# Four attention layers on one core: when pieces of x and the second layer's weights are loaded

## What is computed

```python
x = _L0_xattn_ref(x, ctx, mask, ...)   # q k v projections, softmax(q k^T / 4) v, @ Wo.T, + x, layernorm
x = _L1_xattn_ref(x, ctx, ctx, ...)    # the same with other weights
x = _L2_xattn_ref(ctx, x, ...)         # layernorm + causal self-attention, layernorm + cross-attention,
                                       # layernorm + relu feed-forward 256 -> 1024 -> 256
x = _L3_xattn_ref(x, ctx, ...)         # layernorm, ternary weights (bit_quant), cross-attention, + x
```

## Time and profile before

| | us |
|---|---|
| median of 3 runs | 1397.14 (1395.04 to 1398.23) |
| the profiled execution | 1397.33 |
| its span in the trace | 1395.6 |
| PE busy | 1329.5 (95%) |
| DVE, ACT, POOL busy | 994.2, 898.1, 603.0 |

### The profile page before, as it was taken

One profiled execution on the slowest core, in us unless ns is written; L12 is line 12 of the kernel. 1 busy time (PEld: TensorE's weight loads), 2 busy tenths in 40 slices (PEclk: granted clock), 3 DMA queues, 4 the chain that ended last, 5 costly groups with the idle time before them and its releaser, 6 DMA issues.

```text
span 1395.6 us, 46148 instructions
## 1 busy us (share of the span) xinstructions
PE 1329.5 (95%) x20076; PEld 1138.8 (82%) x20076; DVE 994.2 (71%) x1842; ACT 898.1 (64%) x1519; POOL 603.0 (43%) x767
## 2 busy tenths in 40 slices
PE   5999999999999999999999999999999999899997
PEld 4777888777887878888788878888999999778885
DVE  4778777888788777767776788886664446767774
ACT  4777777777777756666566776776434435667764
POOL 4944544576644643443334342222686665111100
PEclk9999999999999999999999999999999999999999
DMA  7211100010100000000000110000000000001000
GB/s 283 76 31 35 31 13 10 24 31 25 38 9 9 10 25 3 3 2 2 3 2 25 33 31 16 9 9 24 9 9 1 2 1 15 10 32 39 17 25 32
DMA packets 16609, 35.11 MB, mean 25 GB/s; under 512 B 2071, under 2 KB 7447, under 8 KB 15895
## 3 DMA queue, kind: packets, MB, share of 16 engines
q1 hardware_dynamic: 16407, 32.16, 7.1%
HBM read 27.96 MB, written 4.19 MB: 23 GB/s over the span
## 4 chain that ended last, share of the span: by engine, by line
PE 67%; DVE 14%; ACT 8%; POOL 5%; issue 3%; DMA 2%; SPq 0%; DVEq 0%; POOLq 0%; ACTq 0%
DVE s_nm L1101 9%; PE ps L717 8%; PE ps L782 8%; PE ps L744 6%; PE ps L796 6%; PE ps L810 6%; PE ps L606 5%; PE ps L659 5%; PE ps L761 5%; PE ps L631 4%; ACT s_PU L952 4%; PE ps L618 4%; PE ps L595 2%; PE ps L722 2%; DVE s_KH L1058 2%
## 5 line engine op out<-in xcount | busy, mean ns | idle before, releaser
L1101 DVE TENSOR_REDUCE s_nm<-ps 128x8 fp32r<-128x960 f32 (+1 forms) x352 | 395.8, 1168 | 88.4 <-PE ps L659 51.0
L952 ACT ACTIVATE s_PU<-ps 120x1024 f32<-120x1024 f32 (+1 forms) x288 | 280.6, 1024 | 105.5 <-PE ps L722 105.3
L717 PE MATMUL ps<-s_Qs,s_KH 32*120 32x256 f32 (+2 forms) x4608 | 184.8, 288 | 6.4 <-ACT s_PU L952 2.6
L1225 POOL TENSOR_TENSOR s_xs<-s_xs,s_rowv 128x512 f32<-128x512 f32 x96 | 123.9, 1291 | 151.8 <-ACT s_nt L857 133.6
L717 PEld LDWEIGHTS ps<-s_Qs,s_KH 32*120 32x120 f32 (+1 forms) x4608 | 151.5, 181 | 28.4 <-issue 5.1
L1254 POOL TENSOR_SCALAR s_rs<-s_mv 128x2 f32<-128x2 f32 x96 | 23.2, 242 | 325.4 <-DVE s_mv L1138 319.8
L961 ACT ACTIVATE s_Os<-ps 128x512 f32<-128x512 f32 x160 | 95.0, 598 | 102.8 <-PE ps L744 64.2
L782 PE MATMUL ps<-s_W,s_oT 128*128 128x256 f32 x960 | 135.3, 291 | 5.2 <-DVE s_oT L1030 3.5
L606 PE MATMUL ps<-s_xT,s_W 128*128 128x256 f32 x960 | 135.9, 292 | 3.1 <-POOL s_xT L1231 2.8
L744 PE MATMUL ps<-s_PU,s_Vp 120*32 120x256 f32 x2048 | 129.5, 384 | 9.2 <-ACT s_PU L952 7.2
L782 PEld LDWEIGHTS ps<-s_W,s_oT 128*128 128x128 f32 x960 | 120.0, 190 | 16.8 <-DVE s_oT L1030 7.0
(11 more groups left out here) (96 smaller groups left out, 2554.4 us busy)
## 6 DMA issues: line engine op xcount, KB each, us to landing
s_cf<-ctx_t SPq DMA_DIRECT2D x32, 240.0 KB, 2.6
s_ws<-weights SPq DMA_DIRECT2D x28, 256.0 KB, 2.7
s_nt<-x_t SPq DMA_DIRECT2D x16, 256.0 KB, 2.6
s_xs<-x_nat SPq DMA_DIRECT2D x4, 1024.0 KB, 11.3
out<-s_xs SPq DMA_DIRECT2D x16, 256.0 KB, 2.0
s_rowv<-rows SPq DMA_DIRECT2D x6, 512.0 KB, 3.9
s_mi<-mask SPq DMA_DIRECT2D x8, 120.0 KB, 3.4
s_who<-who SPq DMA_DIRECT2D x1, 128.0 KB, 3.2
```

Of the source, the lines that this page charges most:

```text
L717: e.matmul(banks[j][0:n, wide * x:wide * x + wide], kz[row[j], lk, g, c, k0:k0 + n], q[row[j], lq, g, qs_], start=(x == 0 and y_ == 0), st ...
L952: t = e.activation(P_of(i, k)[0:n, :, :], pair("B", i, k)[0:n, :, :], ACT.Exp, scale=0.25)
L1101: e.tensor_reduce(o, v, AX.X, ALU.max, negate=True).then_inc(sem["max"])
L1225: e.tensor_tensor(xs[:, b, :, :], xs[:, b, :, :], row2(layer, 0), ALU.add).then_inc(sem["pool"])
```

## The change

Two lists of predecessors are added in the planner and two settings are replaced.

- Piece 0 of x is put behind stage K.0, and piece k behind stage A of item 4k - 4 (A.0, A.4, A.8).
- Quarter m of L1's weights is put behind A of item 4 + m.
- All of `WANT` (the due-time offsets of every stage in every layer) is replaced, and `STAY` goes from 0.236 to 0.224.

No stage, no instruction of a stage and no semaphore wait is written anew.

```diff
-WANT = dict(Xl=-8.6, xT=-3, cT=-4, mi=-4, bo=(-0.05, 0.32, 4.13, 3.45, 8.95, -1.6), N=(0, 0, 6.16, 6.96, 8.36, 7.97),
...
+WANT = dict(Xl=-16.43, xT=-3, cT=-4, mi=-4, bo=(0.97, -1.34, -3.22, 0.61, 12.29, -3.48), N=(0, 0, 10.64, 12.42, 13.44, 15.82),
...
-STAY = 0.236
+STAY = 0.224
...
     for k in range(4):
-        p.add("SP", "x", k, want=-1 + 1.2 * k)
+        p.add("SP", "x", k, want=-1 + 1.2 * k, after=[("A", 4 * k - 4, 0)] if k else [("K", 0, 0)])
...
         for m in (1, 0, 2, 3) if n == 0 else range(4):
             at = start + .5 * m if n else {1: -9, 0: -3.9, 2: -2.7, 3: -.5}[m]
-            p.add("SP", "ws", layer, m, want=at, rings=[("ws", (layer, m), [(rest_of(layer), layer, m)])])
+            p.add("SP", "ws", layer, m, want=at, after=[("A", 4 + m, 0)] if layer == "L1" else [], rings=[("ws", (layer, m), [(rest_of(layer), layer, m)])])
```

More of the change, by code:

```diff
@@ new lines @@
+WANT = dict(Xl=-16.43, xT=-3, cT=-4, mi=-4, bo=(0.97, -1.34, -3.22, 0.61, 12.29, -3.48), N=(0, 0, 10.64, 12.42, 13.44, 15.82),
+            T=(0, 0.13, 0.21, -0.79, -0.22, 0.31), Q=(1.81, 1.08, 0.96, 0.51, 0, 1.71), Qh=(-0.74, 0.6, -6.57, -3.9, 0, 0.97),
+            Ql=(-0.59, 3.99, 10.39, 2.06, 0, 1.73), K=(2.63, 1.19, -2.71, -0.39, 0, 0.98), Kh=(0.11, -16.63, 4.49, 3.4, 0, 0.76),
+            Kl=(5.54, 8.06, 1.45, 6.65, 0, 7.2), K0=(-13.91, 8.99, 3.75, -3.34, 0, -10.45), V=(3.07, 1.25, 1.38, 0.83, 0, 1.91),
+            Ve=(1.65, -1.23, 1.72, -2.43, 0, -2.35), mf=13, A=(0.29, -1.85, -1.85, -0.06, 0, -3.8),
+            max=(9.11, -12.31, -2.63, -4.61, 0, -2.63), M=(-16.49, -3.61, -3.9, -2.29, 0, -18.15),
+            mTe=(11.14, 12.03, -0.16, 11.27, 0, 8.12), B=(-7.63, -1.62, -2.03, 0.48, 0, -9.14),
+            exp=(-3.12, 14.76, -1.95, 3.12, 0, 13.36), cap=-12.12, PV=(2.26, -0.16, -0.07, 1.54, 0, 1.6),
+            PVe=(-3.45, 1.58, -1.77, 10.39, 0, -0.05), ON=(4.19, 1.38, 3.31, 2.6, 0, -2.95),
+            ONe=(-1.24, -7.63, -1.04, -2.21, 0, -8.35), OT=(3.58, -9.96, 2.54, 2.48, 0, 5.52), O=(-7.31, -5.09, 0.12, 1.33, 0, 1.98),
+            y=(3.96, -9.58, -3.69, 15.16, 2.84, 1.03), st=(5.2, 11.02, 19.36, 14.14, 14.68, 0),
+            rs=(9.18, -8.49, -2.17, -8.62, -2.02, 0), ln=(8.94, -0.06, 0, 0, 0, 0), lng=(-25.75, -16.59, 0, 0, 0, 0), F1=-0.24,
+            Fa=-8.05, Fv=21.82, Hl=-3.15, F2=2.37, out=2.2, Th=(-4.04, -13.24, -7.11, -0.2, -8.86, -15.35),
+            Tl=(0, -2.6, 4.26, -6.59, -10.81, -3.43), OTh=(-15.58, -4.22, -23.32, 2.17, 0, -4.46),
+            OTl=(-2.73, 3.61, 0.93, -0.17, 0, -5.85), Ch=(11.16, 3.48, 0, 4.99, 0, -6.26), Cl=(-7.06, 0.87, 0, -4.91, 0, -4.66))
```

## The result

The changed kernel takes 1401.97 us (median of 7 runs, 1400.48 to 1404.55) against 1397.61 (7 runs, 1395.04 to 1399.02) for the kernel before on the same chip: the ratio is 1.0032, with a 95% interval of 1.0020 to 1.0043. It is slower by about 4 us, where 1393.0 was forecast, and outside the range of 1387.5 to 1398.0.

What follows compares the result with a forecast made beforehand. PE was taken to bound the kernel, with gains only out of its 66 us of idle time. From 1397.33, -3.5 (start), 0 (turn) and -0.8 (end) gave 1393.0 us, range 1387.5 to 1398.0.

Steps and rivals of the forecast that it cites:

- The turn: Turn from L0 to L1: 3.2 us of idle time moves from 275-325 to 225-275 us; 0 net, bounds -3 and +4.
- the start: Start of the kernel, through item 0's exp and PV: -3.5 us carried, with bounds of -1.5 and -6.
- Pieces of x moved back: Start: L0's quarter 3 and xT.2 land 1.25 us earlier, so Q.2 starts at 21.8, not 23.07.
- L1's quarter out of ACT's way: Start, ACT: Qh.2 starts at 24.3; item 0's last maxima end at 28.2, before at 33.19; gain 5.0 us.
- SELF's quarters in their place: Start: SELF's quarters 0 and 1 are folded ahead of item 0's exp, which starts at 32.1, not 35.87; gain 3.8 us.
- first exp after 34 is wrong: Sign at the start: exp of item 0 was expected near 32 us; a start after 34 would show the forecast wrong.
- the slower rival: Turn from L0 to L1: L1's weights arrive last and PE waits for them; 1400.5 us, chance 0.10.
- The end: End of the kernel: more work between A.95.1 and M.95 removes the 0.79 us idle before M.95; -0.8 us.
- Everything else: Rest of the kernel, with stages ordered anew by WANT: 0 us, bounds -5 and +3 for shifts in small gaps.
- more than 43 is wrong: Sign between 32 us and the end: more than 43 us of idle time would show the forecast wrong.

Runs made afterwards that it cites:

- e4: Kernel before with only pieces 1, 2 and 3 of x moved back in SP's order, piece 1 behind L1's quarter 1: 1392.43 us, 0.9965.
- e8: As e4, against before, but with piece 1 of x behind xT.4 in SP's order: 1392.54 us, 0.9963.
- e12: The same kernel as e8, run once more on another chip: 1392.30 us, 0.9967 against before.
- e2: Changed kernel with six dense identity products added on PE in the wait before M.17, nothing else: 1396.86 us, 0.9996 against before.
- e10: Changed kernel with dense products ahead of SELF's first fold and before M.17, and CROSS's wa earlier on DVE: 1394.92 us, 0.9990 against before.

## Why the prediction was wrong, point by point

In short, two terms failed. The turn was priced at 0 by its idle time alone, since "a gain can only come out of those 66 us" of idle time and the busy time was taken as fixed; PE's busy time grew by 7.3 us at a lower clock instead. And the start, -3.5, brought the first exp 0.13 us sooner, not 3.8.

- **Pieces of x moved back: right.** Q.2 starts at 21.79 (predicted 21.8). Moving the pieces alone, without the other half, gave 4.2, 5.7 and 4.7 us by the medians of e4, e8 and e12 (1396.65 - 1392.43, 1398.20 - 1392.54, 1396.97 - 1392.30); I had carried 3.5 for the start. That the two agree is partly luck, since up to 2.3 to 3.6 us of it are the clock, which I had not counted.
- **L1's quarter out of ACT's way: right.** Qh.2 at 24.76 (24.3), item 0's last maxima end at 28.6 (28.2), and ACT's longest wait for a quarter in the first 45 us is 2.0 us, that for the very first quarter at 4.07 us (asked was under 2); it was 3.5:

```profile
ACT s_W L1001 <- DMA s_ws<-weights: 3.8, 3, 2.0
```

- **SELF's quarters in their place: this step failed.** I had B.0 done at 32.1 and exp right behind, 3.8 us gained; it was 35.74, 0.13 gained. The fold was to begin at M.0's end, 28.6, and began at 30.05: 1.45 us late, because K.2, V.2 and A.1.0 keep PE busy until M.0 starts at 29.77. The price of the fold came from the earlier trace rows, where it stands amid full-clock work with free banks. Here it took 0.95 + 0.84 of wait + 1.85, 1.8 us more than the 1.84 counted, because M.0's bank is freed by an ACT that stands at a transfer, and because of the clock. B.0 took 2.1 us at half clock (from 33.62 to 35.69), not 1.7. These three make the 3.6 us. I counted every instruction of the moved fold, but not PE's own queue ahead of it, the bank that it needs, nor the clock. The test "first exp after 34 is wrong" fell as stated.
- **The turn: the idle time moved as said, but more of it, and the term failed.** 275 to 325 idles 0.90 us (predicted 1 to 2; before 4.38), 225 to 275 idles 6.41 (3 to 4; before 0.81), +2.1 us net, inside -3 to +4. Q.16 and K.16 (the two rows below) start without a wait, so the slower rival by its own mechanism, L1's weights last to arrive, isn't what happened; that its 1400.5 us lies near the measured time is luck.

```profile
224.40 1.67 PE L607 MATMUL ps<-s_xT,s_W 128*128 128x256 f32 x12
...
227.13 1.61 PE L619 MATMUL ps<-s_cT,s_W 128*128 128x240 f32 x12
```

  What the term lacked is the clock. A wait isn't only its own length. The two gaps at the turn were followed by 13.65 us of low clock, at most 6.8 us of time; filling one of them gave 5 us back. This is the largest missing term.
- **The end: right.** The 0.79 us ahead of M.95 are gone, and the idle time of the last stretch is 6.57 us against 7.6.
- **Everything else, 0 with -5 and +3:** idle time between 32 us and 1366 is 42.26 against 43.0, which the test "more than 43 is wrong" let pass. Busy time wasn't in the tests, and it was busy time that grew.

From the measured pieces: the profiled execution of before, 1397.33, - 3.9 (idle time) + 7.3 (busy time) = 1400.7, and that of after took 1400.61; this is the bookkeeping of the two traces, not a test. The prediction allowed the low clock one place and 0.8 us. Filling the waits gave 5 to 6 us back (by the ratios, 1.0032 for after against 0.9996 for e2 and 0.9990 for e10). Why after with its gaps filled is still not as fast as before with only the pieces moved (0.9963 to 0.9967) stays open.

The Trainium skill, "TensorE: Matmul & The Clock Gate", Part 1, which I had used only for Q.2, holds the answer in general terms: the clock follows recent activity with a phase of its own. The trace agrees: the same order of work at the turn was low for 13.65 us in after and for 20.5 in the kernel with the first gap filled.
